# Moving the last third of ScalarE's side pieces behind the slope copy and the next head's position cut

## The reference, cut to what matters

```python
logits = jnp.einsum('bhqd,bhkd->bhqk', Q, K) / jnp.sqrt(d)
gates = jax.nn.sigmoid(attn_logits)
pos = jnp.flip(jnp.cumsum(jnp.flip(gates, axis=-1), axis=-1), axis=-1)
pos = jnp.minimum(pos, npos_max - 1)
pos_ceil, pos_floor = jnp.ceil(pos).astype(jnp.int32), jnp.floor(pos).astype(jnp.int32)
logits_int = jnp.einsum('bhqd,dn->bhqn', query, pos_emb)
w = pos - pos_floor
cope = take_along_axis(logits_int, pos_ceil) * w + take_along_axis(logits_int, pos_floor) * (1.0 - w)
scores = jax.nn.softmax(logits + cope, axis=-1)
...
h1 = jnp.einsum('td,efd->etf', xt, w1) + b1[:, None, :]      # feed-forward, 8 experts and a shared one
h3 = jnp.einsum('td,efd->etf', xt, w3) + b3[:, None, :]
a = swiglu(h1 * h3)
```

## Time and profile before

| | |
|---|---|
| median of 3 runs | 5252.0 us (5251.74 to 5252.87) |
| the profiled execution's own time | 5251.89 us |
| its span, first to last instruction | 5250.2 us |
| PE / PEld busy | 3337.5 / 2217.6 us |
| DVE busy | 3946.1 us |
| ACT busy | 2428.4 us |
| POOL busy | 1397.6 us |
| mean granted PE clock | 0.715 of full |
| first slot's masks to last slot's masks | 169.2 to 4989.9 us, so a slot takes about 19 us |

### The profile page before, as it was taken

The page is one execution under the profiler, slowest core; times in us unless marked ns, Lnnn a source line. Parts: engine busy times, 40 slices in busy tenths (PEclk is TensorE's granted clock), DMA queues, the critical chain, the costliest instruction groups (busy, mean ns, idle before and its releaser), DMA issues.

```text
span 5250.2 us, 64557 instructions
## 1 busy us (share of the span) xinstructions
PE 3337.5 (64%) x21126; PEld 2217.6 (42%) x21126; DVE 3946.1 (75%) x8619; ACT 2428.4 (46%) x5505; POOL 1397.6 (27%) x1125
## 2 busy tenths in 40 slices
PE   3347575665757667575665757667575665757676
PEld 2225253443625335353443625335363443525353
DVE  3698687786977778696786968778696776868753
ACT  2454444444444444544444444444544454444432
POOL 0342223223232222223223222222323222222300
PEclk7558586776858668686776858668686776858687
DMA  4000000000000000000000000000000000000000
GB/s 125 8 5 1 1 11 1 11 1 11 1 1 11 1 11 1 1 11 1 11 1 11 1 1 11 1 11 1 3 9 1 11 1 10 1 1 7 1 7 3
DMA packets 42691, 40.93 MB, mean 8 GB/s; under 512 B 6468, under 2 KB 42342, under 8 KB 42360
## 3 DMA queue, kind: packets, MB, share of 16 engines
q1 hardware_dynamic: 42360, 36.85, 2.3%
HBM read 32.64 MB, written 4.19 MB: 7 GB/s over the span
## 4 chain that ended last, share of the span: by engine, by line
DVE 44%; PE 26%; issue 12%; ACT 12%; POOL 3%; DVEq 0%; POOLq 0%; ACTq 0%; DMA 0%; SPq 0%
DVE banks L713 7%; DVE row_negmax L1252 5%; DVE masks L704 4%; PE banks L287 4%; DVE u L941 4%; DVE steps L729 4%; PE banks L356 4%; PE banks L265 3%; PE banks L789 3%; DVE c L675 3%; PE banks L320 3%; DVE eg_eth L959 2%; PE banks L278 2%; DVE o L968 2%; DVE steps L735 2%
## 5 line engine op out<-in xcount | busy, mean ns | idle before, releaser
L618 POOL TENSOR_TENSOR steps<-slope,rises 128x512 f32<-128x512 f32 x256 | 302.6, 1182 | 2951.3 <-DVE masks L704 2357.2
L713 DVE COPY_PREDICATED banks<-masks,banks 128x448 f32<-128x448 int16 (+5 forms) x1536 | 1028.1, 669 | 28.3
L789 PE MATMUL banks<-xn,w 128*128 128x256 f16 x6912 | 852.5, 285 | 111.2 <-ACT h L861 111.2
L789 PEld LDWEIGHTS banks<-xn,w 128*128 128x128 f16 x6912 | 693.7, 102 | 273.8 <-ACT h L861 139.1
L704 DVE TENSOR_SCALAR masks<-shift 128x512 int16<-128x512 int16 x1536 | 334.7, 288 | 438.5 <-ACT shift L546 434.8
L1252 DVE TENSOR_REDUCE row_negmax<-banks 128x4 f32<-128x1024 f32 x256 | 306.1, 1215 | 159.7 <-PE banks L341 159.7
L632 POOL TENSOR_TENSOR partial<-partial,core_scores 128x512 f32<-128x512 f32 x256 | 357.2, 1395 | 0.1
L675 DVE TENSOR_TENSOR_SCAN c<-gate,cap 128x514 f32<-128x514 f32 x256 | 341.6, 1335 | 1.0 <-ACT gate L530 1.0
L443 PE MATMUL banks<-table,core_queries 64*128 64x256 f16 x512 | 124.6, 333 | 339.5 <-ACT slope L593 339.5
L861 ACT ACTIVATE h<-banks,b 128x256 f32<-128x256 f32 x576 | 238.6, 465 | 216.3 <-PE banks L789 216.1
L622 POOL TENSOR_TENSOR partial<-slope,neg_rest 128x512 f32<-128x512 f32 x256 | 330.4, 1291 | 2.1 <-DVE negmax L735 2.1
(11 more groups left out here) (262 smaller groups left out, 7462.7 us busy)
## 6 DMA issues: line engine op xcount, KB each, us to landing
stage<-in_L_ffn_w SPq DMA_DIRECT2D x16, 512.0 KB, 5.5
ahead<-in_ctx SPq DMA_DIRECT2D x32, 128.0 KB, 2.2
ahead<-in_x SPq DMA_DIRECT2D x32, 128.0 KB, 2.3
u<-in_ctx SPq DMA_DIRECT2D x32, 128.0 KB
x<-in_x SPq DMA_DIRECT2D x32, 128.0 KB
out<-x SPq DMA_DIRECT2D x32, 128.0 KB, 1.8
stage<-in_L_ffn_w SPq DMA_DIRECT2D x8, 256.0 KB, 6.1
stage<-in_L_ffn_sw SPq DMA_DIRECT2D x2, 512.0 KB, 4.4
```

Of the source, the lines that this page charges most:

```text
L618: nc.gpsimd.tensor_tensor(k.steps[:, g % 2], k.slope[:], k.rises[:, g % 2], ALU.mult)\
L713: move = nc.vector.copy_predicated(tab[:, :, 0:S - b], k.masks[:, n, :, 0:S - b], tab[:, :, b:S])
L789: last = nc.tensor.matmul(k.bank[bank][:, f * S:(f + 1) * S], w[:, e, a, c, par, f * P:(f + 1) * P], k.x_parts[:, b, c, :], start=(n == 0) ...
```

## The change

On ACT the last third of the slot's side pieces moves from before the slope copy to behind `whole_part(s + 1)`. Nothing is added or removed, no wait changes, and no other engine's program changes.

```diff
@@ core_scalar, after the copy of core_pT
-        for _ in range(pieces - first):
-            next(side)
         if s < G:
             act.wait_ge(sem["core_moved"], s + 1)
             if s >= 1:
                 act.wait_ge(sem["core_steps"], 2 * s)
             nc.scalar.activation(whole(k.slope), k.bank[1][:], ACT.Copy).then_inc(sem["core_slope"], 1)
         if s + 1 < G:
             whole_part(s + 1)
+        for _ in range(pieces - first):
+            next(side)
         for _ in range(ahead_pieces(s)):
             next(ahead, None)
```

## The result

The changed kernel takes 5356.7 us (median of 4 runs, 5354.3 to 5362.4) against 5251.9 for the kernel before (median of 4): ratio 1.0201, 95% interval 1.0183 to 1.0219. It is 105 us slower; I had forecast 85 (5337), in a range up to 5402. The profiled execution took 5356.0 us with a span of 5354.3.

The account below looks back on a forecast made before the run. DVE was taken to bound feed-forward places 1 to 5, and to idle behind ACT and PE in attention places. 5251.9 + 135.8 - 50.9 = 5336.8, said as 5337 us; own range 5295 to 5375, 8-in-10 range 5280 to 5402.

Parts of the forecast that it names:

- The feed-forward term: Places 0 to 5: DVE waits for ACT results made behind the cut, 9.05 us a batch, 135.8 us slower.
- the six steps: Lateness by place: 1.2 us in 0, 1.85 in 1, 1.24 each in 2 and 3, 1.76 each in 4 and 5.
- 1.85 us late: Place 1: DVE's copy L997 starts 1.85 us late, through the chain of L877 and PE's L819.
- third rival: Places 1 to 5: one more slow PE clock stretch each, 63 us on top, 5400 us; chance 0.13.
- The attention term: Places 6 to 15: slope and cut come earlier, 50.9 us faster in sum; bounds 0 and 434.8.
- 8 to 10: Attention places 8 to 10: side piece L1273 in place 10 comes 1.3 us earlier, a gain of 1.3 a batch.
- 13 to 15: Attention places 13 to 15: `table` and the side-head chain come earlier, a gain of 1.6 us in each of 14 batches.
- 6 and 7: Place 6: `table` no longer waits 1.42 us for the slope, but only 0.2 us a batch is left as gain.
- DVE would stay early: Places 8, 9, 13, 14: mask waits go for good, 5170 us with half of them, 4953 with all; chance 0.08.
- the feed-forward's pieces are covered: Feed-forward places: DVE's pieces cost nothing and only the gains stay, 5201 us; chance 0.05.
- Losses and gains: Whole kernel: feed-forward losses and attention gains could cancel, leaving the time the same; chance 0.04.
- my own sum: Whole kernel: feed-forward loss less attention gain, 5337 us, own range 5295 to 5375; chance 0.70.

Follow-up runs that it names:

- e1: Kernel before, with the last third of ACT's side pieces moved behind the cut in places 0 to 5 only: 5403.4 us, ratio 1.0293.
- e3: Kernel before, with the last third of ACT's side pieces between slope copy and cut in all places: 5181.5 us, ratio 0.9868.
- e7: Changed kernel plus 30 PE matmuls, result never read, in place 1 ahead of the wait for the routing copy: 5356.4 us, ratio 1.0202.
- e4: Changed kernel with the routing-weight copy L877 made one piece earlier, ahead of the slope in place 1: 5349.9 us, ratio 1.0187.
- e2: Kernel before, with the last third of ACT's side pieces moved behind the cut in places 6 to 15 only: 5205.1 us, ratio 0.9915.
- e5: e2 with PE's `table` ahead of the last third of PE's side pieces in places 8, 9, 13 and 14: 5275.6 us, ratio 1.0050.
- e6: Kernel before, with the last third between slope and cut only in places 6, 8 to 10 and 12 to 15: 5199.5 us, ratio 0.9902.
- e10: e8 with the 16 added matmuls in place 14 only: 5151.0 us, ratio 0.9810.
- e8: e6 plus 16 PE matmuls, result never read, in each of places 9 and 14: 5159.7 us, ratio 0.9826.

## Why the prediction was right, and where it was off

**The feed-forward term: right in kind, 12% too small.** I had 9.05 us a batch (135.8 in all); places 0 to 5 of the changed kernel cost 10.3, and e1 alone +153. The mechanism is shown three times over: the waits of 1.22 and 1.74 in front of L941, e1's total, and e3, in which the same pieces stand ahead of the cut and the loss falls to 2.1. Five of the six steps were within 0.2 us. The mis-sized term is place 1: "1.85 us late", measured 2.76. The chain was right (1.82 in e7); PE's clock level was not in the term, though the prediction named it as open behind its sum, with 4 us of idle PE in front of L819 (3.88 measured). With the level's 0.94 beside the chain's 1.82 place 1 is accounted for, and e4, which takes both away, fits: 0.94 and the 0.48 by which the chain exceeds the 1.34 of place 2 make 1.42, and it won 1.41. That third rival had priced the clock at 63 us; in places 0 to 5 it came to 0.94 x 15 = 14.

**The attention term: right in sum, by errors that cancel.** I had -3.5 us a batch; it was -3.6, and e2's total -45 against my -50.9. That the sum came out is luck, for the parts did not fit: 8 to 10 brought 2.4 instead of 1.3, 13 to 15 1.2 instead of 1.6, and 6 and 7 lost 0.2 where I had a gain of 0.2. For 6 and 7 the trace has the reason in the batch shown. After `table`, PE's two next groups took 1.88 and 1.94 us in the changed kernel:

```profile
2435.64 1.88 PE L407 MATMUL banks<-first,ahead 128*128 128x8 f32 x8
2437.45 1.94 PE L356 MATMUL banks<-core_pT,core_v 128*32 128x256 f32 x16
```

and 1.06 and 1.07 in the one before:

```profile
2385.05 1.06 PE L407 MATMUL banks<-first,ahead 128*128 128x8 f32 x8
2386.03 1.07 PE L356 MATMUL banks<-core_pT,core_v 128*32 128x256 f32 x16
```

The step that failed here is the silent one: I moved every chain of PE by a constant and left its durations as they were. For 8 to 10 the clock fits too (0.62 against 0.59 in the windows), but no run parts it from an error of mine in following the slots, so that stays open.

Places 13 to 15 came near the forecast for another reason than mine. In the kernel before seven batches of 14 took 56.5 us and seven 54.7; the slot that I followed lay in one of the 56.5 kind. In the changed kernel 13 took 54.1 to 54.3, and one took 56.6. Against the quick kind, at about the same grant (0.65 and 0.66), the gain is thus 0.5 us, not 1.6; the rest is that the slow kind all but went. That it went is tied to the order: e2, e4 and e7, with the pieces behind the cut and PE's order as before, had one, none and none of 14; e1, with ACT's old order in these places, had five. But the way there was PE's level ahead of `table`, shown above, and not the shorter queue alone.

**Two of my own tests came out against me.** The first move was to wait 2.8 us for `table` in place 13; it waited 1.1 in twelve batches of 14 (1.14 in eleven of them). And I wrote that the masks "should hardly wait for L546 any more"; 229.4 us of 434.8 are left, and they stand in places 9 and 14, at 7.0 and 8.4 us, rather more than before. My working had the reason and I did not read it off: in these places ACT's first two thirds and the copy of `core_pT` come late by themselves, and the slope and the cut are queued behind those. The part of the edit that works is in 6, 8 and 13.

**The rivals.** That DVE would stay early is out by e5, which even took the wait for `table` away. That the feed-forward's pieces are covered is out by e1. Losses and gains stayed far from cancelling.

**The range.** The range of my own sum, 5295 to 5375, does not follow from the two bounds given for it: the attention term between 0 and twice 50.9, and 15% of 135.8, make 5266 to 5408. The measured 5356.7 lies in both.

## What to carry to other kernels

Before moving an instruction of an in-order engine back behind other work, look what reads its result: a result that had lain ready for microseconds cost 1.2 to 1.8 us a slot once it was made behind an instruction that waits for the very engine that reads it. To stop just ahead of that wait was the best order that ran (e3, -69 us). To do so only in the places that had gained took the feed-forward's losses away, but the kernel was 18 us slower than e3 (e6), its attention places all at the lower grant. And where PE idles in a large part of each slot, compare batches of one run before believing a gain: the same program there differed by 3 us of 54 with the granted clock, and 16 matmuls in one gap (e10 against e6, 48 us) were worth as much as the reordering that they were added to (e6, 51 us), though less than e3's 69.

## What the runs showed of the hardware

I had not expected the granted clock to move time about between edited and unedited places. In e5 places 13 to 15 took 53.8 or 56.8 us with nothing else different, in e3 51.3 or 54.5, in the kernel before 54.7 or 56.5, nearly by turns from batch to batch. PE was at its low level (half rate, 1.2 GHz) all through places 8 and 12 of the kernel before (grant 0.50), and at the high one (2.4 GHz) for most of places 1 to 5 (0.93). Matmuls whose result nobody reads raised the grant of the place they stood in, 0.79 to 0.91 in place 1 (e7) and 0.62 to 0.89 in place 14 (e10), and shortened it by 0.9 and 3.0 us; in place 9 the grant rose too, 0.69 to 0.81 (e8), and the place got 1.2 us longer by their wait. The Trainium skill, "TensorE: Matmul & The Clock Gate" (Part 1: The HAM clock gate), has it that activity releases the throttle and idleness brings it back; these runs agree. What I can't derive is which batch of a run gets which grant, and so why e6 fell on the slow side in all of its batches and e3 in half of them. So a gain of 20 us from an edit in this kernel may come with the grant and not with the queue that the edit was made for.
